# A DLRM tower on one core: the GpSimd queue's gathers and weight sums in another order, two weight loads behind waits, register reads spread

## The reference

```python
e = stack([tbl_f[ids[:, f]] for f in range(8)], axis=1)      # 512 x 8 x 1024, f32
t = tanh(relu(e[:, not_idx] @ Wn1 + bn1) @ Wn2 + bn2)        # not_idx = [2, 3]
iv = e with fields not_idx replaced by t
pair_fuse = relu(concat(iv[pairs[:,0]], iv[pairs[:,1]]) @ W1 + b1) @ W2 + b2
sum_res = pair_fuse(and_pairs).sum(1) + pair_fuse(or_pairs).sum(1) + remaining fields
z = sum_res / count
h = relu(concat(z, dense_ctx) @ W_top1 + b_top1)             # 1040 -> 512
y = relu(h @ W_top2 + b_top2) @ W_top3                       # 512 -> 256 -> 1
```

## Time and profile before

| | us |
|---|---|
| median of 3 runs | 554.11 |
| the 3 runs | 554.11, 556.40, 553.35 |
| the profiled execution | 555.12 |
| its span, first to last instruction | 553.3 |

### The profile page before, as it was taken

How to read it: one execution, slowest core, us unless ns; L and a number is a source line. 1 busy time by engine, 2 the same in 40 slices (tenths; PEclk the granted TensorE clock), 3 DMA queues, 4 the chain that set the end, 5 groups by cost and what they waited for, 6 DMA issues and landing times.

```text
span 553.3 us, 6173 instructions
## 1 busy us (share of the span) xinstructions
PE 533.0 (96%) x2392; PEld 441.2 (80%) x2392; DVE 357.8 (65%) x370; ACT 248.1 (45%) x301; POOL 234.2 (42%) x176
## 2 busy tenths in 40 slices
PE   5799969899899999999999999999999999999998
PEld 5698848778688888888888788888888888888885
DVE  5367899799766686788746688852423784345832
ACT  3375277365456634444444645331335432142343
POOL 5408888569817636022077107855545400000000
PEclk9799989999999999999999999999999999999999
DMA  7917866582596576369089435999999983331000
GB/s 254 330 44 175 160 168 201 167 178 89 125 213 184 145 105 181 94 95 153 18 170 300 160 103 154 267 248 247 247 246 248 247 247 105 97 108 39 0 1 0
DMA packets 38607, 87.31 MB, mean 158 GB/s; under 512 B 4305, under 2 KB 4561, under 8 KB 38578
## 3 DMA queue, kind: packets, MB, share of 16 engines
q0 software_dynamic: 18624, 49.29, 41.2%
q1 hardware_dynamic: 19522, 37.51, 21.3%
q10 hardware_dynamic: 432, 0.11, 0.1%
HBM read 86.90 MB, written 0.00 MB: 157 GB/s over the span
## 4 chain that ended last, share of the span: by engine, by line
PE 81%; DVE 6%; POOL 4%; DMA 2%; issue 2%; ACT 2%; another core or an unknown queue 1%; DVEq 0%; ACTq 0%
PE PS L1063 78%; POOL XR L483 4%; DMA XR<-table,rows 2%; DVE XR L890 2%; DVE WO L797 1%; PE PS L1092 1%; ACT WO L591 1%; PE PS L1241 1%; DVE XR L965 1%; DVE XR L942 1%; PE PS L1213 1%; DVEq L389 0%; DVE XO L873 0%; DMA XR<-ints 0%
## 5 line engine op out<-in xcount | busy, mean ns | idle before, releaser
L1063 PE MATMUL PS<-XO,WO 128*128 128x512 f32 (+1 forms) x2256 | 510.5, 388 | 11.6 <-DVE WO L797 8.7
L1063 PEld LDWEIGHTS PS<-XO,WO 128*128 128x128 f32 x2256 | 420.3, 190 | 99.8 <-DVE WO L797 11.5
L591 ACT ACTIVATE WO<-WR 128x1024 fp32r<-128x1024 f32 x93 | 98.6, 1060 | 240.1 <-PE PS L1063 220.8
L797 DVE TENSOR_TENSOR WO<-WR,WO 128x1024 fp32r<-128x1024 f32 x93 | 113.7, 1222 | 141.4 <-ACT WO L591 126.2
L483 POOL DMA_INDIRECT XR<-table,rows x96 | 127.5, 1328 | 60.0 <-issue 28.3
L621 ACT ACTIVATE XO<-XR 128x1024 fp32r<-128x1024 f32 (+1 forms) x76 | 79.3, 1046 | 9.9 <-DVE XR L942 7.9
L505 POOL DMA_DIRECT2D WR<-weights x30 | 37.4, 1657 | 98.6 <-DVE WO L797 54.1
L873 DVE TENSOR_TENSOR XO<-XR,XO 128x1024 fp32r<-128x1024 f32 x60 | 73.0, 1217 | 1.0 <-ACT XO L621 0.5
L568 POOL DMA_INDIRECT XR<-table,rows_rest x32 | 55.5, 1735 | 39.0 <-DMA XR<-table,rows_rest 36.6
L890 DVE STREAM_TRANSPOSE XR<-XR 128x1024 f32<-128x1024 f32 x26 | 55.7, 2149 | 3.5 <-DMA XR<-table,rows 3.5
L942 DVE TENSOR_TENSOR XR<-XR 128x1024 f32<-128x1024 f32 (+1 forms) x32 | 38.6, 1219 | 0.0
(11 more groups left out here) (72 smaller groups left out, 117.5 us busy)
## 6 DMA issues: line engine op xcount, KB each, us to landing
WR<-weights SPq DMA_DIRECT2D x71, 512.0 KB
WR<-weights POOLq DMA_DIRECT2D x30, 512.0 KB, 7.4
XR<-table,rows POOLq DMA_INDIRECT x110
XR<-table,rows_rest POOLq DMA_INDIRECT x32, 12.7
XR<-dense_t SPq DMA_DIRECT2D x3, 32.0 KB, 3.1
XR<-w_dense SPq DMA_DIRECT2D x3, 32.0 KB, 3.0
XR<-ints SPq DMA_DIRECT2D x1, 84.0 KB, 2.1
XR<-identity ACTq DMA_DIRECT2D x1, 64.0 KB, 2.9
```

The source lines that it names most:

```text
L591: nc.scalar.activation(WO[:, n % 2, 0, :], WR[:, slot, :], ACT.Copy).then_inc(w_hi, 1)
L797: V_.tensor_tensor(WO[:, n % 2, 1, :], WR[:, raw_slot(n), :], WO[:, n % 2, 0, :].bitcast(FP32), ALU.subtract).then_inc(w_lo, 1)
L1063: mm = nc.tensor.matmul(PS[:, bank, cols], WO_t[:, slot, ws, i, k, :], XO[:, x0 + k, xs, cols], start=first and k == 0 and n == 0, stop=la ...
```

## The change

It does four things.

- GpSimd's queue: all but two of field 2's sixteen calls now stand ahead of the sums for stage 0's Q6, those sums are followed at once by Q7's, and the first half of field 3 comes before P4's. Field 4's second half comes ahead of the sums for stage 1's Q5 instead of behind them.
- SyncE: the loads of pieces 2 and 3 wait until the whole-row half of the second field has landed, the load of piece 8 until the rest of the second field has.
- The registers: instead of six reads at t = 24, ACT and DVE read two at t = 38, two at t = 40 and two at t = 42.
- No instruction is added or removed on PE, and no transfer is added or removed.

```diff
--- before.py
+++ after.py
@@ -213,6 +213,9 @@
 
 TURNS_AT = {1: (3, 4), 2: (13, 15, 17, 19), 3: (22, 23, 25, 27), 4: (35, 37, 39, 41),
             5: (55, 56, 59, 60), 6: (95, 99, 103, 107), 7: (111, 112, 117, 119)}
+
+
+REGS_AT = {38: (2, 3), 40: (4, 5), 42: (6, 7)}
 
 
 def sum_done(s, which, half, kk):
@@ -438,8 +441,12 @@
                 sp.dma_start(raw_piece(2 + h), quadrant_rows(4 + 2 * h, 0)).then_inc(raw_in[2 + h], 16)
                 for b in range(2 * h, 2 * h + 2):
                     sp.wait_ge(x0_in[b], 16)
+
+            for b in range(2):
+                sp.wait_ge(x1_in[b], 16)
             load(2)
             load(3)
+            sp.wait_ge(field1_in[1], 16 * 4)
             load(8)
             for n, split in ((9, 2), (12, 3), (13, 8), (16, 9), (14, 10), (15, 11), (17, 12), (20, 13), (28, 14),
                              (29, 15), (21, 16), (24, 17), (25, 20), (32, 21),
@@ -513,23 +520,22 @@
             pool.wait_ge(rows1_ready, 1)
             for i in range(2):
                 gather_quarter(i)
-            for h in range(2):
-                add_piece(0, Q6, h)
             pool.wait_ge(rows2_ready, 1)
             gather_half(2, 0)
-            for h in range(2):
-                add_piece(0, Q7, h)
-            gather_half(2, 1, range(4))
+            gather_half(2, 1, range(6))
+            for j in (Q6, Q7):
+                for h in range(2):
+                    add_piece(0, j, h)
+            gather_half(2, 1, range(6, 8))
+            gather_half(3, 0)
             for h in range(2):
                 add_piece(0, P4, h)
-            gather_half(2, 1, range(4, 8))
-            gather_half(3, 0)
             gather_half(3, 1)
             pool.wait_ge(setup_done, 1)
             gather_half(4, 0)
+            gather_half(4, 1)
             for h in range(2):
                 add_piece(1, Q5, h)
-            gather_half(4, 1)
             add_piece(1, Q7, 0)
             for h in range(2):
                 add_piece(1, Q6, h)
@@ -732,9 +738,9 @@
                         for h in range(2):
                             act.wait_ge(t1_sum, h + 1)
                             nc.scalar.activation(WR[:, 2 + h, :], WR[:, h, :], ACT.Copy).then_inc(t1_copy, 1)
-                    if t == 24:
+                    if t in REGS_AT:
                         act.wait_ge(setup_done, 1)
-                        regs.update(pair_regs(act, range(2, SLOTS)))
+                        regs.update(pair_regs(act, REGS_AT[t]))
             evacuate(QUARTERS - 1)
             for n in range(D2 // P):
                 act.wait_ge(top2_done, n + 1)
@@ -1034,9 +1040,9 @@
                     for at, key, i in SUMS:
                         if at == t:
                             operand_sum(*key, i)
-                    if t == 24:
+                    if t in REGS_AT:
                         dve.wait_ge(setup_done, 1)
-                        regs.update(pair_regs(dve, range(2, SLOTS)))
+                        regs.update(pair_regs(dve, REGS_AT[t]))
                     if e in (TOP - 2, TOP - 1):
                         add_rest(4 * (e - TOP + 2) + m)
                     if FIRST[Z] <= t < FIRST[Z] + 8:
```

## The result

The changed kernel is slower: 565.85 us, the median of 4 runs (565.42 to 569.18), against 554.70 of the kernel before on the same chip. The ratio is 1.0215, 95% interval 1.0176 to 1.0254. So it is slower beyond the noise, by about 2%. The profiled execution took 569.18 us, 14.1 more than the profiled one of before (555.12); it is the slowest of the four and lies 3.3 us above their median, so the losses read from it are somewhat larger than those of a typical run.

What follows compares the result with a forecast made beforehand. PE alone bounds the kernel from 151.67 us on, so gains lie in its earlier waits. From the profiled 555.12 us, 1.83, 0.22 and 2.35 were subtracted, giving 550.7 us, range 546.5 to 555.

Steps and rivals of the forecast that it cites:

- The start: PE's first matmuls, 19.86 to 24.06 us and the half-clock ones behind: bounds -6.0 to +4.9 us, taken as 0.
- the stutter: PE at 19.86 to 24.06 us: five matmuls in 4.2 us, a gap ahead of each, while DMA engines are full.
- D: Rival: field 2's gathers prolong the start's stutter by 4.9 us, plus 2.4 of half clock; 558.0 us, chance 0.06.
- The late count at t = 28: PE's count reached ACT and DVE some 5 us late; not touched by the edit, not expected again: -2.35 us.
- Field 4 ahead of the sums: Field 4's gather lands before its transposes at t = 42: gain 1.83 us, and 0.2 us shortly behind.
- ACT's 8.03 us: ACT's wait until 155.02 for stage 1's Q6 summed weights, queued behind field 4's gather; claimed to go, with 0.2 us.
- 13 us of cover: POOL's forecast time left between field 4's last gather, at 98 us, and the start of Q5's sums at 111.6.
- Q6's sums cost nothing: Stage 0's Q6 sums, behind fourteen mostly landed calls, are issued when they were: cost 0.
- Registers and SyncE's waits: Spread reads at t = 38 to 42 cost 0 to 0.4 us each beyond cover; delayed weight loads 0; both taken as 0.
- t = 16 and 18: PE's gaps of 3.83 and 0.71 us at weight splits, DVE being short of time; expected to stay as before.
- The gather calls that are held: POOL's 11.60 us call at 118.69, read as DVE's fp32 operations with two SBUF inputs holding its issue.
- Rival E: No effect: transfers queued by the sums hold the gather call, or register reads delay DVE; 554 to 555 us, chance 0.09.

Runs made afterwards that it cites:

- before_again: The kernel before, unchanged, run and profiled again on another chip; 555.85 us (one run).
- e5: The changed kernel with eight instead of fourteen of field 2's gather calls ahead of the sums for Q6 and Q7; 561.13 us, ratio 1.0065.
- e7: The kernel before plus twenty plain 128 KB loads in 1 KB rows on SyncE's queue, which field 2's gathers wait for; 577.86 us.
- e8: The kernel before plus fourteen plain 128 KB loads on POOL's queue, where the change has field 2's gathers; 561.71 us.
- e6: The changed kernel, with POOL waiting for the second field before field 2's calls and for landing after each four of them; 561.53 us.
- e13: e11 with one pause per eight calls in fields 3 and 4 and one per four in slots 5, 6 and 7; 545.87 us, ratio 0.9854.
- e14: e13 with the start of the kernel before, so without pauses at the start; 552.99 us, ratio 0.9969.
- e10: The kernel before plus a wait for landing after each four calls of slot 3's second and slot 4's first half; 556.94 us, ratio 1.0026.
- e9: The kernel before, with each group of the start's quarter-row gathers waiting for a whole-row gather of the second field; 564.04 us.
- e2: The changed kernel with field 2's gathers and stage 0's sums put back in the order of before; 553.48 us, ratio 1.0181.
- e12: The changed kernel with pauses at the start, after field 2's last call and in fields 3 and 4, four field 2 calls ahead of the sums; 573.59 us, ratio 1.0384.
- e1: The kernel before with only field 2's gathers and stage 0's sums in the new POOL order; 547.75 us (one run).
- e1_again: The same kernel as e1, run on another chip; 571.90 us (one run).
- e11: e10 plus two pauses in the start's gather stream, before and between the second field's quarter-row groups; 559.20 us (4 runs).

## Why the prediction was wrong

I forecast 550.7 us in a range of 546.5 to 555; the median is 565.85. Behind the start the sum came out: 4.4 us forecast as gained, 5.1 measured. The start, which I put at 0, cost 19.2.

**The start, the step that failed.** I bounded the start by the time that the DMA engines are full: "If the stutter lasts while DMA is full". The upper bound from it was +4.9 us, 7.3 with the slow clock (D), and I gave it 0.06. Measured: +19.2 us. What failed is the choice of the cause, and with it the bound. In the trace of before two things stand beside the stutter, the full DMA engines of the earlier trace rows and POOL's stream of gather calls, which runs from 4.3 to 21.8 us (its last call is in the earlier trace rows), and I looked at the first alone. The earlier trace rows doesn't show the second plainly: POOL is busy at 16 to 18 us, where PE still runs, and idle at 22 to 24, where it stutters. A stream as the cause needs a delay at both ends. It has one: in the kernel before the stutter outlasts the last call by 2.3 us, in before_again, e5 and after by 3.5, 4.0 and 3.6. With the stream as the cause the size comes out right: the change adds fourteen calls to it, 14 x 1.25 = 17.5 us, up to 39.3 by my own sum, and the stutter ended at 43.1. The bytes (e7) and POOL's plain issues beside full engines (e8) don't do it, and in after it goes on with the engines at 0.41 and 0.13; waits for landing inside the stream take it away (e6 for field 2's calls, e13 against e14 for the start's).

**The late count at t = 28.** "I see nothing of the kernel that does this" was wrong: POOL issues a stream without a pause from 96.2 to 107.3 us there, and ACT's wait for the count ends at 109.0. e10 with pauses in this stream has none, e9 and before_again (6.4 us) have it again. Taking the 2.35 us as gained was right in after, but not for my reason: I had no mechanism for it, so that it came true was luck. The likely reason, argued from POOL's timeline alone, is that some of the calls of fields 3 and 4 are held there for 1.4 to 4.4 us, so that no more than five short ones follow each other (nine in the kernel before). Both disturbances that I had left unexplained in the profile of before go with such a stream and go away with its pauses, and the change made the first stream longer.

**Field 4 ahead of the sums.** Right. Q5's sums go when their splits allow (126.52; 111.62 in the earlier trace rows, and the start is 19.2 us later), ACT's 8.03 us and the gaps of 1.83 and 0.2 are gone. The condition, 13 us of cover, is real: in e2 and e12 the cover is gone and the same order costs 5.66 and 13.24 us. What it wins isn't constant either: before_again, the kernel before once more, has no gap at t = 42 to win back.

**Q6's sums cost nothing.** Wrong where the start is clean. The copy for which they wait exists earlier there (34 us in e13), while fourteen calls hold POOL until 42: 1.20 us at t = 12 in e1. In after it was hidden, since the stutter had moved the copy to 59.

**Registers and SyncE's waits.** Nothing stands at t = 38 to 42 in after, so the reads cost what was forecast, 0. The loads of pieces 2 and 3 moved to 20.9 us; e1_again, which has neither of these edits, loses as much as after, so they are no part of the loss. What each alone does wasn't measured.

**t = 16 and 18.** 3.56 us of 3.83 stayed, as forecast; that 0.71 went wasn't.

**The gather calls that are held.** That DVE's operations with two SBUF inputs hold them was an argument of the prediction, not tested by an edit. Calls of 9.5 to 13 us stand in the same place of DVE's list in e2, e11 and e13 (111.90, 9.46 us). But before_again, the same kernel, has the two sums in the same place and no held call; POOL and DVE there:

```profile
119.30 1.38 POOL L483 DMA_INDIRECT XR<-table,rows  x1 [0.30 <-issue]
```

```profile
119.64 1.22 DVE L942 TENSOR_TENSOR XR<-XR 128x1024 f32<-128x1024 f32 x1
121.38 1.22 DVE L797 TENSOR_TENSOR WO<-WR,WO 128x1024 fp32r<-128x1024 f32 x1 [0.52 <-ACT WO L591]
```

DVE does the same operations in the same order, with two idle moments (0.52 us here, 0.81 at 126) where the profile of before has none from 119 to 129. That fits DVE as the cause in part only: the call was through at 120.7, before the first of them. So what holds a call isn't shown. Rival E, the sums ahead of it, fares worse: here the sums are the same and nothing is held, in e2 a call is held 9.54 us with no sum issued in the 40 us before it, and in after the calls behind four sums in a row show no hold of this length (21 calls of 1.375 us mean between 60 and 98).

What stays open: what in the chip couples the calls to PE's counts and its issue (whether the counting, the supply of PE's instructions or something behind both is held up, no run separates), why chip I doesn't show it, from how many calls on, and why the late loss near 310 us comes in some runs only. Streams in which every few calls one takes 2 us or more (61 to 93 us in e13) did no harm.

## What to carry to other kernels

Before a queue's idle time is filled with gathers, look at what the critical engine does while such a stream runs already; if it is slow or its counts are late there, the loss to expect goes by the time that the added calls take (here 1.25 us each), and not by bytes. Where an unexplained wait stands in the profile of before, list all that runs beside it, not only the fullest resource, and look for the same company at the other unexplained places. A queue's idle wait of a few microseconds between gathers can be worth more than what it delays, if each sum or load queued behind it has its cover counted.

## What the runs showed of the hardware that I had not expected

- On four of the five chips, and in the first comparison, an unbroken stream of indirect gather calls, 1.25 us apart, made the semaphore counts of PE reach ACT and DVE late: the count of the transposes at the start by 5.9 us in before, 26.9 in after, 6.9 in e14, and 0.04 in e13, which has the pauses. At the start it also let PE issue a matmul of 0.37 us only each 0.7 to 2.8 us, at the 1.2 GHz level (granted clock 0.50). Plain transfers of the same size, from SyncE or from GpSimd, didn't prolong it.
- On chip I none of the four kernels profiled showed it, e1 beside DMA engines at 1.02 and 368 GB/s; the kernel before took 543.57 us there, which is 10.6 to 17.5 under all the others, and about what e13 took (545.87) on a chip with the effect.
- With a wait for landing after each four to eight calls of the long streams, e13's profile has no such late count left. One wait ahead of eight calls (e9) wasn't enough.
- The same gather call behind the same two sums took 11.60 us in one profile of the kernel before and 1.38 us in the other; what decides it isn't shown.
